# A graph kernel's second attention row stage, done inside the first edge walk

## What is computed

```
def gat_layer(x, W, a_l, a_r, b, src, dst, num_nodes):
    z  = (x @ W).reshape(num_nodes, heads, d)
    el = jnp.einsum('nhd,hd->nh', z, a_l)
    er = jnp.einsum('nhd,hd->nh', z, a_r)
    e  = el[src] + er[dst]
    e  = jnp.where(e > 0, e, NEG_SLOPE * e)
    m  = segment_max(e, dst)
    ex = jnp.exp(e - m[dst])
    alpha = ex / segment_sum(ex, dst)[dst]
    return segment_sum(z[src] * alpha[:, :, None], dst) + b
h = relu(gat_layer(layernorm(x), W1, al1, ar1, b1, ...))   # 2 heads of 128
out = gat_layer(h, W2, al2, ar2, b2, ...)                  # 1 head of 256
```

## Time and profile before

| | us |
|---|---|
| median of 3 runs | 5060.1 |
| lowest and highest | 5054.87, 5061.7 |
| profiled execution, device time | 5045.04 |
| span of the profile | 5043.5 |
| TensorE busy | 3145.1 |
| VectorE busy | 2020.3 |
| ScalarE busy | 802.4 |
| GpSimd busy | 2733.0 |
| mean granted TensorE clock | 0.778 |

### The profile page before, as it was taken

One profiled execution on the slowest core, in us unless ns is written; L12 is line 12 of the kernel. 1 busy time (PEld: TensorE's weight loads), 2 busy tenths in 40 slices (PEclk: granted clock), 3 DMA queues, 4 the chain that ended last, 5 costly groups with the idle time before them and its releaser, 6 DMA issues. The chain is left out here.

```text
span 5043.5 us, 64240 instructions
## 1 busy us (share of the span) xinstructions
PE 3145.1 (62%) x14232; PEld 1998.7 (40%) x14232; DVE 2020.3 (40%) x7896; ACT 802.4 (16%) x2128; POOL 2733.0 (54%) x2821
## 2 busy tenths in 40 slices
PE   4467677666466666666312999116666666563998
PEld 3355555554333333333312778103333333342454
DVE  5466666664244444443830111342212122265233
ACT  2110000001100001010100333110100001153333
POOL 1577777772277777775344000567777777532000
PEclk9787777887677777777556999557777777786999
DMA  5555555553444444443534666554444444353111
GB/s 160 145 146 145 144 146 144 145 145 86 95 127 128 127 128 128 127 129 98 156 116 138 213 215 216 171 148 114 113 113 114 113 114 114 101 138 102 36 51 58
DMA packets 391840, 649.25 MB, mean 129 GB/s; under 512 B 104557, under 2 KB 253087, under 8 KB 390963
## 3 DMA queue, kind: packets, MB, share of 16 engines
q0 software_dynamic: 144160, 410.22, 31.3%
q1 hardware_dynamic: 211842, 200.50, 13.6%
q10 hardware_dynamic: 35728, 37.50, 2.4%
HBM read 513.62 MB, written 134.34 MB: 128 GB/s over the span
## 5 line engine op out<-in xcount | busy, mean ns | idle before, releaser
L507 PE MATMUL walk_ps_part<-walk_rows,walk_whot 128*80 128x129 f32 (+1 forms) x6272 | 1710.0, 427 | 848.8 <-DMA walk_rows<-h,walk_idx 564.4
L507 PEld LDWEIGHTS walk_ps_part<-walk_rows,walk_whot 128*80 128x80 f32 x6272 | 1043.1, 195 | 1353.3 <-issue 594.0
L397 POOL DMA_INDIRECT walk_rows<-z_one_head,walk_idx x784 | 765.5, 976 | 282.3 <-issue 227.9
L397 POOL DMA_INDIRECT walk_rows<-z_two_heads,walk_idx x784 | 767.1, 978 | 238.8 <-issue 235.8
L397 POOL DMA_INDIRECT walk_rows<-h,walk_idx x784 | 742.8, 947 | 257.4 <-issue 237.9
L634 DVE TENSOR_SCALAR walk_whot<-keep_winx,walk_dloc,walk_w 128x80 f32<-128x80 f32 x2352 | 566.3, 331 | 0.0
L432 ACT ACTIVATE walk_window<-walk_ps_part 80x257 f32<-80x257 f32 (+1 forms) x294 | 112.3, 382 | 1809.5 <-PE walk_ps_part L507 1804.8
L630 DVE COPY walk_carry<-keep_carry 80x1 f32 (+1 forms) x245 | 32.2, 151 | 758.4 <-ACT walk_weight L420 758.4
L469 PE MATMUL walk_ps_el_rows<-keep_ident,walk_rows 128*32 128x128 f32 (+1 forms) x98 | 32.3, 329 | 418.6 <-DMA walk_rows<-z_one_head,walk_idx 281.8
L1282 POOL DMA_DIRECT2D y_slots<-exp_y x54 | 38.7, 716 | 413.2 <-DVE exp_y L1348 380.9
L1321 PE MATMUL exp_ps_hid<-exp_hT,exp_w 128*128 128x256 f32 x864 | 220.2, 388 | 20.8 <-DMA exp_b<-in_ffn_b 20.5
(11 more groups left out here) (306 smaller groups left out, 3719.7 us busy)
## 6 DMA issues: line engine op xcount, KB each, us to landing
exp_w<-in_ffn_W SPq DMA_DIRECT2D x108, 512.0 KB
walk_dstB<-dst SPq DMA_DIRECT2D x196, 160.0 KB
agg<-walk_window ACTq DMA_DIRECT2D x198, 80.3 KB
h_slots<-walk_clear SPq DMA_DIRECT2D x98, 148.0 KB
exp_h<-h_slots SPq DMA_DIRECT2D x54, 256.0 KB
y_slots<-exp_y POOLq DMA_DIRECT2D x54, 256.0 KB, 5.8
walk_rows<-z_two_heads,walk_idx POOLq DMA_INDIRECT x784
walk_rows<-z_one_head,walk_idx POOLq DMA_INDIRECT x784
```

Of the source, the lines that this page charges most:

```text
L397: pool.indirect_dma_start(out=Z[k // 2][:, k % 2 * GROUP_TILES + t, :], out_offset=None, in_=table, in_offset=bass.IndirectOffsetOnAxis(ap ...
L507: last = pe.matmul(P[k % 2][0:WIN, cols], S[k % HOTS][:, h, t, :], Z[k // 2][:, k % 2 * GROUP_TILES + t, h * HS:h * HS + HW], start=t == 0 ...
```

## The change

The phase rows2 is taken out of the list. Its work is done in walk1 by a class `SecondRows`, in units of 128 nodes. Unit v is the tile of nodes (v - 3) x 128 (`LEAD = 3`). There are 52 units, 49 with nodes. Units 0 to 48 go with the 49 pairs; the first three of them work on rows behind the table. Units 49 to 51 come behind the walk, in a loop `tail`. The plan compares the first node of certain groups with the tile that will be read; were one too early, all units with nodes would be done again behind the walk. `rowtab` holds each unit's row. The tables for z and er of layer 2 and `agg` get 6656 rows and more; they had 6272, 6352 and 6400. Three small PSUM tiles of the walks share one bank, in both attention walks, which frees banks for the units.

SyncE, per pair, behind its loads:

```diff
+    def load(self, sp, v, k, row, stored, count):
+        if stored is not None:
+            sp.wait_ge(stored, count)
+            sp.sem_inc(self.tick, 1)
+        sp.wait_ge(self.h_ready2, v + 1)
+        sp.dma_start(self.a[k][:, :], self.agg[bass.ds(row, TILE), :]).then_inc(self.agg_in[k], 16)
+    def store(self, sp, v, k, turn, row):
+        sp.wait_ge(self.er_done, v + 1)
+        sp.dma_start(self.table[bass.ds(row, TILE), :], self.z[k][:, :]).then_inc(self.landed[k], 16)
+        sp.dma_start(self.erd[bass.ds(row, TILE), :], self.parts[k][:, :]).then_inc(self.landed[k], 16)
+        sp.wait_ge(self.landed[k], turn * 32 + 32)
+        sp.sem_inc(self.z_free2, 1)
...
                     for m in range(1, PAIRS + 1):
-                        load(i * PAIRS + m, m % 2, i * PAIRS + m)
+                        p = i * PAIRS + m
+                        load(p, m % 2, p)
+                        if node:
+                            node.load(sp, p, m % 2, unit_row(sp, p), stored, i * (32 * PAIRS) + (32 * m - 16))
+                            node.store(sp, p - 1, (m - 1) % 2, i * (PAIRS // 2) + (m - 1) // 2, unit_row(sp, p - 1))
```

The weights' four loads (`start_sp`) are queued behind the first pair's inputs. ScalarE waits for them ahead of its first index copies:

```diff
+    def start_act(self, act):
+        act.sem_inc(self.z_copied1, 1)
+        act.sem_inc(self.hT_ready1, 1)
+        act.wait_ge(self.w_in, 64)
+        act.wait_ge(self.ones_set, 1)
+    def head(self, act, v, k):
+        act.wait_ge(self.turned2, v + 3)
+        act.wait_ge(self.z_done1, v + 1)
+        for hf in range(HALVES):
+            last = act.activation(self.hT[:, hf, :], self.psT[:, hf * TILE:(hf + 1) * TILE], ACT.Relu, bias=self.bcol[:, hf:hf + 1])
+        last.then_inc(self.hT_ready1, 1)
+    def copy_out(self, act, v, k):
+        act.wait_ge(self.z_done1, v + 2)
+        act.wait_ge(self.z_free2, v + 1)
+        act.activation(self.z[k][:, 0:D], self.psZ[:, 0:D], ACT.Copy)
+        act.activation(self.z[k][:, D + 1:D + 3], self.psZ[:, D:D + 2], ACT.Copy).then_inc(self.z_copied1, 1)
...
                 for m in range(PAIRS):
+                    p = i * PAIRS + m
+                    if node:
+                        node.head(act, p, m % 2)
+                        act.wait_ge(node.agg_in[(m + 1) % 2], i * (8 * PAIRS) + 16 * ((m + 1) // 2 + 1))
+                        act.sem_inc(act_tick, 1)
                     window(i * UNROLL + 2 * m, 2 * m, i * (16 * UNROLL) + (16 * 2 * m + 16))
+                    if node:
+                        node.copy_out(act, p, m % 2)
                     if gat:
                         exps(i * PAIRS + (m + 1), (m + 1) % 2)
```

TensorE (the semaphore `h_ready2` begins at 2, so `turn(v)` waits for `scale(v)`):

```diff
+    def turn(self, pe, v, k):
+        pe.wait_ge(self.h_ready2, v + 3)
+        pe.wait_ge(self.hT_ready1, v + 1)
+        for hf in range(HALVES):
+            last = pe.transpose(self.psT[:, hf * TILE:(hf + 1) * TILE], self.h[k][:, hf * 128:(hf + 1) * 128], self.ident[:, :])
+        last.then_inc(self.turned2, 1)
+    def products(self, pe, v, k):
+        pe.wait_ge(self.hT_ready1, v + 2)
+        pe.wait_ge(self.z_copied1, v + 1)
+        for hf in range(HALVES):
+            last = pe.matmul(self.psZ[:, 0:D + 2], self.hT[:, hf, :], self.Waug[:, hf, :], start=hf == 0, stop=hf == HALVES - 1)
+        last.then_inc(self.z_done1, 1)
...
                 products(s, 2 * m, 0)
+                if node:
+                    node.turn(pe, p, m % 2)
                 products(s, 2 * m, 1)
                 products(s, 2 * m, 2)
+                if node:
+                    node.products(pe, p, m % 2)
                 if ahead:
                     turn_el(p + 1, b, turn)
```

VectorE (`scale` and `split` do what those of the row stage did, on one tile; `split` of unit v waits for `copy_out(v)`; `augment` makes the appended weight columns behind the walk's first constants):

```diff
+    def scale(self, dve, v, k, turn):
+        dve.wait_ge(self.agg_in[k], turn * 16 + 16)
+        heads_of = self.a[k][:, :].rearrange("p (h w) -> p h w", w=HEAD_W)
+        dve.tensor_scalar(self.inv[:, :], heads_of[:, :, HEAD_W - 1], 1e-30, None, ALU.max)
+        dve.drain()
+        dve.reciprocal(self.inv[:, :], self.inv[:, :])
+        dve.drain()
+        dve.wait_ge(self.turned2, v + 1)
+        for hf in range(HALVES):
+            dve.tensor_scalar(self.h[k][:, hf * 128:(hf + 1) * 128], heads_of[:, hf, 0:128], self.inv[:, hf:hf + 1], None, ALU.mult)
+        dve.drain().then_inc(self.h_ready2, 1)
...
                 spread(p, q, s, loaded)
                 maxima(p, q)
+                if node and m:
+                    node.split(dve, p - 1, 1 - q)
                 logits(p, m % PAIRS)
                 dve.wait_ge(w_ready, p + 1)
                 hots(s, 2 * m % UNROLL, W[q])
                 hots(s + 1, (2 * m + 1) % UNROLL, W[q])
+                if node:
+                    node.scale(dve, p, q, half)
```

Behind the walk (VectorE shown; the other engines have the same loop). `left` is 1, or 24 if the plan found a group too early:

```diff
+                if node:
+                    node.split(dve, n * PAIRS, 0)
+                    left, first = tail(dve)
+                    u, half = n * PAIRS + 1, n * (PAIRS // 2)
+                    node.scale(dve, u, 1, half)
+                    with dve.Fori(0, left) as i:
+                        node.scale(dve, i * 2 + (u + 1), 0, i + (half + 1))
+                        node.split(dve, i * 2 + u, 1)
+                        node.scale(dve, i * 2 + (u + 2), 1, i + (half + 1))
+                        node.split(dve, i * 2 + (u + 1), 0)
+                    node.split(dve, left * 2 + u, 1)
...
-PHASES = ("plan", "rows1", "walk1", "rows2", "walk2", "post", ...
+PHASES = ("plan", "rows1", "walk1", "walk2", "post", ...
```

More of the change, by code:

```diff
@@ L174, in _ @@
             act.wait_ge(nils, 1)
[L175 to L178, removed]
+            pieces = [(r, min(r + 1280, NODE_ROWS)) for r in range(0, NODE_ROWS, 1280)]
+            for lo, hi in pieces:
+                act.dma_start(dram["agg"][lo:hi, :].rearrange("(p r) w -> p (r w)", p=128),
+                              nil[:, 0:(hi - lo) // 128 * AGG_W]).then_inc(agg_clear, 16)
+            act.wait_ge(agg_clear, 16 * len(pieces))
         @block.gpsimd
@@ L274, in edge_walk @@
+def edge_walk(nc, keep, dram, name, table, heads, nodes=None):
     H, gat = max(heads, 1), heads > 0
@@ L279, in edge_walk @@
     ident = keep["ident"]
+    er_rows = None if not gat else dram["er2"] if H == 2 else dram["er1"]
+    agg = dram["agg"]
     with Phase(nc, name) as ph:
@@ L438, in _ @@
             act.wait_ge(consts, 1)
+            if node:
+                node.start_act(act)
             for s in range(UNROLL):
@@ L452, in _ @@
                     window(i * UNROLL + (2 * m + 1), 2 * m + 1, i * (16 * UNROLL) + (16 * (2 * m + 1) + 16))
+            if node:
+                node.head(act, n * PAIRS, 0)
             window(n * UNROLL, 0, n * (16 * UNROLL) + 16)
+            if node:
+                node.copy_out(act, n * PAIRS, 0)
             window(n * UNROLL + 1, 1, n * (16 * UNROLL) + 32)
+            if node:
+                left, first = tail(act)
+                u = n * PAIRS + 1
+                node.head(act, u, 1)
+                node.copy_out(act, u, 1)
+                with act.Fori(0, left) as i:
+                    for k in range(2):
+                        node.head(act, i * 2 + (u + 1 + k), k)
+                        node.copy_out(act, i * 2 + (u + 1 + k), k)
             act.wait_ge(stored, n * (16 * UNROLL) + 48)
@@ L463, in _ @@
             pe.wait_ge(consts, 1)
+            if node:
+                node.start_pe(pe)
             def turn_el(p, b, turn):
@@ L541, in _ @@
                 pair(n * PAIRS, 0, n * UNROLL, None, False)
+                if node:
+                    left, first = tail(pe)
+                    u = n * PAIRS + 1
+                    node.turn(pe, u, 1)
+                    node.products(pe, u, 1)
+                    with pe.Fori(0, left) as i:
+                        for k in range(2):
+                            node.turn(pe, i * 2 + (u + 1 + k), k)
+                            node.products(pe, i * 2 + (u + 1 + k), k)
             else:
@@ L561, in _ @@
                 dve.memset(wsb[k][:, :], 0.0)
+            if node:
+                node.start_dve(dve)
             dve.drain().then_inc(consts, 1)
+            if node:
+                node.augment(dve)
             def spread(p, q, s, loaded):
@@ L731, in attention_rows @@
     ident = keep["ident"]
-    table, erd = dram[f"z{heads}"], dram[f"er{heads}"]
-    with Phase(nc, f"rows{layer}") as ph:
+    table, erd = dram["z2"], dram["er2"]
+    with Phase(nc, "rows1") as ph:
         Waug = ph.sb("w", [128, HALVES, AW])
@@ L910, in split @@
                 dve.drain().then_inc(er_done, 1)
-            if first:
-                pipeline(dve, (normed, 1), (split, 0))
-            else:
-                pipeline(dve, (scale, 1), (split, 0))
+            pipeline(dve, (normed, 1), (split, 0))
 def after_attention(nc, io, keep, dram):
```

217 lines of the change are left out of this document (160 added, 57 removed).

## The result

The changed kernel takes 5423.6 us (median of 4 runs, 5419.3 to 5428.8), the kernel before in the same session 5057.7 (4 runs): a ratio of 1.0724, interval 1.0707 to 1.0741. It is slower, as forecast, but by 366 us instead of 95, and outside my range of 5050 to 5265.

A forecast was written before the change was run, and what follows sets the result against it. GpSimd's gathers bound walk1 at 20.5 us a pair; the change makes it 24.5, between two chains. 48(P - 22.5) gives +96; 5045 + 96 + 15 = 5156, said 5155. Range 5085 to 5230 (0.59), wider 5050 to 5265 (0.79).

The forecast's parts named there:

- I take 4, the middle: SyncE's wait for a unit's two stores to land: 4 us, between bounds of 1.5 and 7.5.
- rival 3: SyncE's landings in walk1 near the upper bound: P = 28.5, +288 us, 5348; chance 0.07.
- P: Time of one pair in walk1, between score transposes: 24.5 us forecast, 20.49 before, break-even at 22.5.
- the upper bound: Landing of a unit's stores at 7.5 us, the old stage's wait per 448 rows; it makes SyncE's chain 28.5.
- SyncE's chain, 25.0: A pair in walk1: stores, landing, loads, spread, maxima, `split`; 25.0 us, or 22.5 and 28.5 with the landing's bounds.
- The aggregate tile: Its load, landed about E+19.7, releases ScalarE's window copy 1 us after TensorE would; next E by that way at 24.4.
- E: Zero point of a pair's sums: VectorE finishes `split` of unit p-1 in pair p and starts the logits.
- The loop between TensorE and VectorE, 24.0: In walk1, one-hots, products, scores, maxima, with TensorE standing 3.2 us for the unit's scaling: 24.0 us a pair.
- Rival 2, the lower clock: TensorE stays at the lower clock all pair in walk1: P = 26.6, +197 us, 5257; chance 0.14.
- Start, +21: Weight loads awaited ahead of index copies delay walk1's first gather from 160.52 to 181.5, first score transpose to 206.6.
- End, 65.5: From walk1's last score transpose to walk2's first gather, with three units behind the last window: 65.5 us, 183.4 before.
- Rival 1, the unit fits under the gathers: The unit's work fits in walk1 and GpSimd stays the bound: P = 20.6, -91 us, 4969; chance 0.12.

The follow-up runs named there:

- e1: Changed kernel with the landing of a unit's stores waited for one unit later: 5231.3 us, ratio 1.0368 to before; on a slower chip 6462.1, 1.0659.
- e9: e7 with SyncE's order changed, a pair's inputs loaded one step earlier, ahead of the previous unit's store: 5089.4 us, ratio 1.0077 to before.
- e4: Changed kernel without ScalarE's wait for the next unit's aggregate tile ahead of the window copy: 5280.9 us, ratio 1.0467 to before.
- e5: Changed kernel with TensorE's transposes and products of a unit moved later in its queue: 5411.3 us, ratio 1.0713 to before.
- e10: e7 with both TensorE's later transposes and products and SyncE's earlier input loads: 4942.6 us, ratio 0.9794 to before.
- e7: Changed kernel with e1 and e4 together, and ScalarE's wait for the unit's weights behind the first index copies: 5134.6 us, ratio 1.0177 to before.
- e10_all: The e10 kernel, both orders changed on e7, run on a slower chip: 6017.3 us, ratio 0.9979 to before.

## Why the prediction was wrong, step by step

- **"I take 4, the middle"**, the landing of a unit's stores, is the step that failed. It is my rival 3, P = 28.5 and 5348, to which I gave 0.07, and the measured time lies above even that. `er`, 128 rows of 6 bytes, lands after 7.0 us, nearly the 7.5 that SyncE waited per chunk of 448 rows, while the 129.5 KB of `z` land after 3.7. I scaled the landing with the rows, and argued against the upper bound with that. The measurement contradicts it: the small transfer is the late one, and the earlier trace rows already named `er` as the one waited for. The Trainium skill (DMA: Bandwidth & Descriptors, Anatomy of one DMA) has a formula, for transfers that GpSimd issues, from which I estimate 2.0 us for `er` and 2.3 for `z`; these stores are issued by SyncE, and the medians agree with neither.
- **SyncE's chain, 25.0.** Measured in the profile after (means over 25 pairs, 400 to 1200 us): stores issued 1.3 (1.2 forecast), then 9.05 to the next inputs (4), loads 8.3 (9.75), to the spread 3.3 (3.4), to the first scan 0.8 (1.0), to the end of `split` 7.6 (5.7). Sum 30.3 against 25.0, and 30.3 is the pace of this stretch (29.88 over the whole walk). So 5.0 us of the excess lie ahead of the next inputs and 1.9 in the way to `split`; the loads took 1.5 less. The landing is 7 to 8 with register work, and the turn of SyncE's loop adds some 4 us to it in every fourth pair, 1 in the mean, which no term of mine held. e1 shows the landing's part, and e9 that the long pair goes when the turn is out of the way.
- **The aggregate tile.** I saw that its load releases ScalarE's window copy, but priced this at 24.4 from a landing at E+19.7. Its load is issued 20.5 us after E (where `split` ends) in the mean and takes 4.7 instead of the 3.4 taken. That delays `copy_out` and `split`; without it (e4) the chain is 2.2 us shorter.
- **The loop between TensorE and VectorE, 24.0**: right within half a microsecond. e9, where it is the loop that shows, has 23.52, with the stand of 2.7 us.
- **Rival 2, the lower clock**: not what cost the time. Between the two score transposes after, the granted clock was 0.65 in the mean, against 0.78. But VectorE waited for inputs in those pairs, and moving TensorE's stand (e5) brought the granted clock back to 0.72 while P stayed at 29.77. So a higher clock alone bought nothing here. In e10 it was 0.82 between the same two transposes. All of these are mixtures of 1.2 and 2.4 GHz.
- **Start, +21**: e7 undoes it and wins 20.1 us at the first score transpose. In the profile after, that transpose is 27.1 us late, and 7.8 of these lie ahead of walk1's first load (171.90 for 164.15). In the changed kernel run again this load is only some 2.4 us late. I had 0 to 1 for all that stands ahead of the walk; what it is was not tried. **End, 65.5**: 78.4. The first tail load is issued 9.0 us after the last window copy (1680.10 to 1689.06), where I had 2.2: it stands behind the landing of the stores before it, the same mis-sized term. With that wait moved (e1) the end takes 71.5 us, against 76.8 in the changed kernel beside it.
- **Rival 1, the unit fits under the gathers** (4969, 0.12): false for this kernel. The work itself does fit on a usual chip: e10 does all of it at 20.50. What doesn't fit is where it stands in two queues.

After these runs the pace on a usual chip is accounted for: from 29.55 to 24.65 by e1 and e4 together (3.24 and 2.26 alone), and 4.15 more by the two orders.

My number for P, 24.5, is near e7's 24.65, but that is no support for it: it is the pace of another kernel, without the two waits.

## What to carry to other kernels

Before work is moved into a loop, list every in-order queue it enters and ask what each of its waits holds back there. Here a stage of 153 us was moved under other work and 366 us were lost. With the same work in another order, two waits moved and one left out, 109 were won. Price a landing by the nearest row for its kind, not by its bytes, and keep a completion wait behind the loads that the next iteration needs. When two loops have nearly the same length, test both edits together before calling either useless. And look at what the turn of each engine's loop costs in the profile once its body has grown.

## What the runs showed of the hardware

- A store of 128 rows of 6 bytes (0.8 KB) landed after 7.0 us in the median, 128 rows of 1 KB beside it after 3.7.
- A turn of SyncE's loop can cost microseconds in its queue: 7.55 us from `er` to `dstB` instead of 1.95 in the two pairs of e7 shown above, 5.4 of them between the branch and the next instruction. It is not so for every loop. In the kernel before, a turn of walk1 has 250 instructions of SyncE in the trace, and 0.2 to 0.3 us pass behind the branch; after, it has 338, and 3.8 to 5.1 us pass. In walk2 of the profile after it has 194, and 0.2 us pass. VectorE shows the same: 327 to 329 instructions and under 0.1 us before, 399 and 3.0 to 3.6 us in walk1 after, 251 to 253 and under 0.1 us in walk2. The costly turns are the long ones; that the length is the cause is likely but no run changed it alone.
- Chips differ by 20%. VectorE's one-hots, from 500 us, in e1 on a slower chip (over 1000 us) and on a usual one (over 800 us):

```profile
L880 DVE TENSOR_SCALAR walk_whot<-keep_winx,walk_dloc,walk_w 128x80 f32<-128x80 f32 x802 | 216.5, 337 | 176.8 <-issue 176.6
```

```profile
L880 DVE TENSOR_SCALAR walk_whot<-keep_winx,walk_dloc,walk_w 128x80 f32<-128x80 f32 x960 | 231.5, 334 | 0.0
```

  One instruction takes as long on both, but on the slower chip 176.6 us pass before them with no releaser, 7 us a pair, and none on the other. In e10_all, on another slower chip, there is no such gap, but 224.7 us in 1000 pass ahead of VectorE's logits, where e10_again has 18.2 in 600. SyncE's issues in e1 on the slower chip have gaps too: `dstB` to `erw` to `reset` at 845.50, 849.03 and 853.26 in one pair, where the next three are 0.5 us apart. What the gaps are was not tested.
